# A fused cross-attention and expert block: some 128x128 transposes leave TensorE, are done as 32x32 blocks on VectorE and put in place through DRAM; PSUM banks come from one table, and each engine has a new order

## The reference

```python
# layer 1, on hidden = layernorm(x)
q = hidden @ Wq.T + bq;  k = ctx @ Wk.T + bk;  v = ctx @ Wv.T + bv     # 16 heads of 32
scores = clip(q @ k.T / sqrt(32), -50, 50);  masked keys to -10000, then clipped again
probs = softmax(scores);  probs = probs / (sum(probs) + 1e-8)
delta = clip(residual_scale, 0, 0.3) * (probs @ v @ Wo.T + bo)
x = x + (delta - mean) / sqrt(var + 1e-5) * ln_gamma + ln_beta
# layer 2, on n = layernorm(x)
weights = softmax(n @ router_w.T)                     # 8 experts, the best 2 are kept
h = einsum('bth,eih->beti', n, down_w);  a = silu(h)  # 16 hidden values for each expert
x = x + sum over the kept experts of weight * (a @ up_w.T)
```

## Time and profile before

| what | before |
|---|---|
| time, median of 3 runs (lowest to highest) | 189.34 us (188.48 to 189.62) |
| span of the profiled execution, first to last instruction | 187.4 us |
| TensorE busy | 180.4 us (96% of the span) |
| VectorE busy | 126.2 us (67%) |
| ScalarE busy | 111.4 us (59%) |
| GpSimd busy | 89.2 us (48%) |
| granted TensorE clock | 1.00 throughout |
| hardware DMA queue, share of 16 engines | 31.4% |

### The profile page before, as it was taken

One profiled execution on the slowest core, in us unless ns is written; L12 is line 12 of the kernel. 1 busy time (PEld: TensorE's weight loads), 2 busy tenths in 40 slices (PEclk: granted clock), 3 DMA queues, 4 the chain that ended last, 5 costly groups with the idle time before them and its releaser, 6 DMA issues.

```text
span 187.4 us, 3699 instructions
## 1 busy us (share of the span) xinstructions
PE 180.4 (96%) x1308; PEld 135.8 (72%) x1308; DVE 126.2 (67%) x294; ACT 111.4 (59%) x231; POOL 89.2 (48%) x149
## 2 busy tenths in 40 slices
PE   7999999889999999999999999999999999999972
...
GB/s 167 308 396 166 310 380 297 1 3 87 157 13 10 149 195 0 14 115 0 0 0 17 126 112 3 2 2 17 114 14 112 3 75 37 3 106 119 170 95 297
DMA packets 12290, 19.66 MB, mean 105 GB/s; under 512 B 2416, under 2 KB 4464, under 8 KB 12272
## 3 DMA queue, kind: packets, MB, share of 16 engines
q1 hardware_dynamic: 12272, 19.43, 31.4%
...
## 4 chain that ended last, share of the span: by engine, by line
PE 91%; DVE 4%; ACT 2%; issue 1%; POOL 0%; ACTq 0%; POOLq 0%
PE ps_r L434 52%; PE ps_v L434 8%; PE ps_t L459 8%; PE ps_r L513 5%; PE ps_v L540 4%; PE ps_v L527 4%; PE ps_r L489 4%; PE ps_v L499 4%; PE ps_v L590 3%; DVE xs L1175 2%; ACT stage L767 2%; ACT q_sb L753 0%; DVE hidt_lo L1063 0%; DVE hidden L1166 0%; ACT hidden L806 0%
## 5 line engine op out<-in xcount | busy, mean ns | idle before, releaser
L434 PE MATMUL ps_r<-wo_hi,attt_hi 128*128 128x512 f32 x64 | 26.3, 411 | 0.0
L434 PE MATMUL ps_r<-hst_hi,wq_hi 128*128 128x512 f32 x64 | 25.9, 404 | 0.4 <-ACT stage L767 0.4
L434 PE MATMUL ps_r<-hst_hi,wq_lo 128*128 128x512 f32 x64 | 25.3, 395 | 0.0
L434 PE MATMUL ps_r<-wo_hi,attt_lo 128*128 128x512 f32 x64 | 25.3, 395 | 0.0
L434 PE MATMUL ps_r<-hst_lo,wq_hi 128*128 128x512 f32 x64 | 25.2, 394 | 0.0
L434 PE MATMUL ps_r<-wo_lo,attt_hi 128*128 128x512 f32 x64 | 25.2, 394 | 0.0
L1445 POOL TENSOR_TENSOR xs<-xs,beta_bc 128x512 f32<-128x512 f32 x16 | 21.2, 1346 | 5.5 <-DMA beta_bc<-beta 5.5
L1449 POOL TENSOR_TENSOR attt_lo<-wk,attt_hi 128x512 fp32r<-128x512 f32 x16 | 21.2, 1335 | 4.4 <-ACT attt_hi L780 4.4
L747 ACT ACTIVATE hs<-xs,ln_bias,ln_rstd 128x512 f32<-128x512 f32 x16 | 12.7, 812 | 14.9 <-POOL ln_bias L1437 14.9
L1101 DVE TENSOR_SCALAR stage<-stage,exp_max 128x1024 f32<-128x1024 f32 x16 | 15.0, 935 | 9.0 <-ACT stage L767 8.7
L767 ACT ACTIVATE stage<-ps_r 128x1024 f32<-128x1024 f32 x16 | 16.1, 1025 | 5.4 <-PE ps_r L513 5.4
...
## 6 DMA issues: line engine op xcount, KB each, us to landing
...
```

What stands on the lines that cost most here:

```text
L434: last = pe.matmul(dst, w, m, start=start and i == 0, stop=stop and i == n - 1, skip_group_check=unseen)
```

## The change

Three things change together.

1. Batches 2 and 3 no longer have `hs_transpose`, and the pairs of tiles in `MOVED` (batches 0, 1 and 2, whole) no longer have `x1_transpose`. In their place VectorE turns each 32x32 block of the tile (`hs_turn`, `x1_turn`, one instruction a tile, from SBUF to SBUF). A block then still stands in the wrong group of 32 partitions. SP writes the turned tiles to DRAM (`hs_send`, 1 MB for a batch; `x1_send`, 512 KB for a pair) and reads them back in four DMAs, one for each 32 partitions (`hs_fetch`, `x1_fetch`), which puts the groups in place. ScalarE then makes `hst_hi` from SBUF, and GpSimd, not VectorE, makes `hst_lo`; `x1t` is copied by ScalarE from the fetched tiles.
2. The eight PSUM banks are one table, `BANKS`: each string is one bank, with its uses in order. Every kind has semaphores of its own for full and free.
3. The lists of all five engines are written anew. `spread` is cut in `spread_out` and `spread_in`, and small per-tile results have a slot for each batch, which takes two kinds of wait away from ScalarE (`projected_squares`, `x1_squares`).

```diff
+BANKS = (
+    "K0 Q01 S02 S06 Q13 S14 Q21 W03 Q30 S26 W12 S32 S36 W23 W30 U11 U22 U33",
+    "K1 Q02 S03 S07 S10 S15 Q22 Q23 S20 Q31 S27 W13 S33 S37 U00 W31 U12 U23",
+    "K2 Q03 S04 Q11 S11 S16 W00 S21 W10 Q33 S30 S34 W21 U02 W33 U20 U31",
+    "K3 S00 S05 Q12 S12 S17 W01 S22 S24 W11 S31 S35 W22 U03 U10 U21 U32",
+    "h01 h03 Q00 S01 Q10 S13 Q20 W02 S23 S25 Q32 W20 U01 W32 U13 U30",
+    "V0 h11 s00 v01 m0 s10 v11 s20 v21 f00 f02 a00 v30 v33 f12 f21 n30 f30 a21 a31",
+    "V1 h12 s01 v02 s11 v12 s21 v22 f01 s30 s31 v31 f10 f13 a10 f22 n31 a20 n33 f33",
+    "h00 h02 h10 h13 v00 v03 v10 v13 v20 v23 f03 a01 v32 f11 f20 a11 f23 n32 f31 f32 a30",
+)
+
+MOVED = ((0, 0), (0, 1), (1, 0), (1, 1), (2, 0), (2, 1))
+
+MOVED_HS = (2, 3,)
+
+LOW_ON_VECTOR = ()
+
...
+        hs_turned = sb("hs_turned", [P, KC * S])
+        x1_turned = sb("x1_turned", [P, 2, 2 * H])
+        hs_of = hs_turned[:, :].rearrange("p (q c t r) -> p t c q r", q=4, c=KC, t=NT)
+        x1_of = x1_turned[:, :, :].rearrange("p j (q c t r) -> p j t c q r", q=4, c=KC, t=2)
+
+        hs_back = hs[:, :, :].rearrange("p q (c t r) -> p q c t r", c=KC, t=NT)
+
+        x1_fetched = x1_turned[:, :, :].rearrange("p j (q n) -> p j q n", q=4)
+        x1_back = x1_turned[:, :, :].rearrange("p j (q c t r) -> p j t c q r", q=4, c=KC, t=2)
 
...
+            def hs_send(b):
+
+                sp.wait_ge(hs_turn_ok, NT * (MOVED_HS.index(b) + 1))
+                sp.dma_start(hs_scratch[:, :], hs_turned[:, :]).then_inc(hs_sent, 16)
+
+            def hs_fetch(b):
+                sp.wait_ge(hs_sent, 16 * (MOVED_HS.index(b) + 1))
+                for a in range(4):
+                    sp.dma_start(hs[32 * a:32 * (a + 1), :, :], hs_blocks[:, :, a, :]).then_inc(hs_moved, 16)
+
+            def x1_send(b, j):
+
+                sp.wait_ge(x1_turn_ok, 2 * (MOVED.index((b, j)) + 1))
+                sp.dma_start(x1_scratch[j, :, :], x1_turned[:, j, :]).then_inc(x1_sent[j], 16)
+
+            def x1_fetch(b, j):
+                sp.wait_ge(x1_sent[j], 16 * (b + 1))
+                for a in range(4):
+                    sp.dma_start(x1_fetched[32 * a:32 * (a + 1), j, :, :], x1_blocks[j, :, :, a, :]
+                                 ).then_inc(x1_moved[j], 16)
 
             def store(b, t):
-                sp.wait_ge(u_free, ring_r.count(f"U{b}{t}"))
...
+            hs_send(2)
+            spread_out(0, 0)
+            spread_in(0, 0)
+            hs_fetch(2)
             load(3)
-            spread(1, 1)
-            spread(2, 0)
-            spread(2, 1)
-            spread(3, 0)
-            spread(3, 1)
+            spread_out(0, 1)
+            spread_in(0, 1)
+            hs_send(3)
+            hs_fetch(3)
+            spread_out(1, 0)
+            spread_out(1, 1)
+            spread_in(1, 0)
+            spread_in(1, 1)
...
                 pe.wait_ge(hs_ok, NT * b + t + 1)
-                transposes(f"h{b}{t}", chunks(hs, t))
+                transposes(f"h{b}{t}", chunks(hs, t), h_full)
...
                 if m == 0:
-                    pe.wait_ge(hst_ok, ring_t.count(f"h{b}3"))
+                    dve, pool = hs_low(b + 1)
+                    pe.wait_ge(hst_ok, dve)
+                    if pool:
...
             def hs_hi(b, t):
                 if b:
-                    act.wait_ge(mm_full, ring_r.full(f"Q{b - 1}3"))
-                hi(f"h{b}{t}", hst_hi[:, t, :, :], hst_hi_ok)
+                    act.wait_ge(q_full, banks.count(f"Q{b - 1}3"))
+                if b not in MOVED_HS:
+                    hi(f"h{b}{t}", h_full, hst_hi[:, t, :, :], hst_hi_ok)
+                else:
+                    act.wait_ge(hs_moved, 64 * (MOVED_HS.index(b) + 1))
+                    act.copy(hst_hi[:, :, :, 32 * t:32 * (t + 1)].rearrange("p t c r -> p c t r"), hs_back[:, t, :, :, :]
+                             ).then_inc(hst_hi_ok, 1)
...
             def x1_out(b, t):
-                hi(f"n{b}{t}", x1t[:, t, :, :], x1t_ok)
+                if b:
+                    act.wait_ge(f_full, NT * (b - 1) + t + 1)
+                j = t // 2
+                if (b, j) in MOVED:
+                    act.wait_ge(x1_moved[j], 64 * (b + 1))
+                    act.copy(x1t[:, t, :, :].rearrange("p c (q r) -> p c q r", q=4), x1_back[:, j, t % 2, :, :, :]
+                             ).then_inc(x1t_ok, 1)
+                else:
+                    hi(f"n{b}{t}", n_full, x1t[:, t, :, :], x1t_ok)
...
             def hs_lo(b, t):
-                lo(f"h{b}{t}", hst_lo[:, t, :, :], hst_hi[:, t, :, :], hst_hi_ok, NT * b + t + 1,
-                   hst_ok)
+                if b not in MOVED_HS:
+                    lo(f"h{b}{t}", hst_lo[:, t, :, :], hst_hi[:, t, :, :], hst_hi_ok, NT * b + t + 1, hst_ok)
+                else:
+                    dve.wait_ge(hst_hi_ok, NT * b + t + 1)
+                    of_quarter = slice(32 * t, 32 * (t + 1))
+                    dve.tensor_tensor(hst_lo[:, :, :, of_quarter].rearrange("p t c r -> p c t r"), hs_back[:, t, :, :, :],
+                                      hst_hi[:, :, :, of_quarter].rearrange("p t c r -> p c t r").bitcast(F32),
+                                      ALU.subtract).then_inc(hst_ok, 1)
+
+            def hs_turn(b, t):
+
+                dve.wait_ge(hs_ok, NT * b + t + 1)
+                if MOVED_HS.index(b):
+                    dve.wait_ge(hs_moved, 64 * MOVED_HS.index(b))
+                dve.transpose(hs_of[:, t, :, :, :], hs[:, t, :]).then_inc(hs_turn_ok, 1)
+
+            def x1_turn(b, t):
+
+                j = t // 2
+                dve.wait_ge(x1_ok, NT * b + t + 1)
+                if b:
+                    dve.wait_ge(x1t_ok, NT * (b - 1) + 2 * j + 2)
+                dve.transpose(x1_of[:, j, t % 2, :, :, :], xs[:, NT * b + t, :]).then_inc(x1_turn_ok, 1)
 
...
+            def hs_lo(b, t):
+                pool.wait_ge(hst_hi_ok, NT * b + t + 1)
+                of_quarter = slice(32 * t, 32 * (t + 1))
+                pool.tensor_tensor(hst_lo[:, :, :, of_quarter].rearrange("p t c r -> p c t r"), hs_back[:, t, :, :, :],
+                                   hst_hi[:, :, :, of_quarter].rearrange("p t c r -> p c t r").bitcast(F32),
+                                   ALU.subtract).then_inc(hst_pool_ok, 1)
...
             tile_stats(2, 2)
+            tile_stats(2, 3)
+            clip(0, 0)
             hs_lo(1, 0)
             hs_lo(1, 1)
-            clip(0, 0)
+            hs_lo(1, 2)
             clip(0, 1)
-            hs_lo(1, 2)
             hs_lo(1, 3)
-            centre_experts()
+            hs_turn(2, 0)
+            hs_turn(2, 1)
+            hs_turn(2, 2)
+            hs_turn(2, 3)
+            reciprocals(0, 0)
+            centre_wo(2)
+            centre_wo(3)
             clip(0, 2)
-            reciprocals(0, 0)
             clip(0, 3)
-            tile_stats(2, 3)
```

939 lines of the change are left out of this document (475 added, 464 removed), and 4 rows, old and new, of the table RING_R.

## The result

| | before | after |
|---|---|---|
| time, median (lowest to highest) | 189.34 us (188.48 to 189.62) | 198.36 us (196.74 to 199.44) |
| ratio, 95% interval | | 1.048 (1.042 to 1.053) |
| profiled span | 187.4 us | 197.1 us |
| TensorE idle within the span | 7.0 us | 18.8 us |
| time lost to a lower granted clock | 0 | 7.4 us |

Slower by 4.8%, where I had forecast 2.6% faster. The last two rows are sums over slices of 1 us: what TensorE was not busy, and each slice's length times what its granted clock lacked of 1.00. Further down, a median is over all runs of a kernel, and a ratio leaves out runs over 1.5% longer than its fastest one (3 of e5's ten, 2 of e17's four, one each of e3's four and e10's six).

The account below looks back on a forecast made before the run. TensorE bounds the kernel, VectorE its end: `project(3, 3)` at 168.84 − 10.3 − 3.0 + 3.1 + 2.0 = 160.6, plus 3.5 + 15.7 + 2.7 gives a span of 182.5, plus 1.9 gives 184.4 us; range 179.5 to 190.5.

Parts of the forecast that it names:

- a microsecond of TensorE work taken away is a microsecond won: First matmul to 177.2 us: the chain hardly leaves TensorE, so removed work counts in full if no other engine is awaited.
- 10.3 us in full: Twenty transpose groups off TensorE: ten at 0.59, eight at 0.44, 0.9 for two more, all ahead of `project(3, 3)`.
- the term 3.1 + part of 2.0: New TensorE waits: 3.1 us before `scores(1, 1)` for batch 2's trip, 2.0 us for the other trips and short waits.
- Batch 2's own wait: Before `scores(1, 1)`: TensorE asks at 56.5, ScalarE frees the banks at 59.6, a wait of 3.1 us, bounds 0 and 6.
- hidden with a cover of 1 us: Batch 3's trip: tiles back by 77.0, `hs_lo(3, 3)` ends near 87, `query(3, 0)` comes at 88.3, so no wait.
- My own last sentence: Sign of being wrong: a first large wait at batch 3's queries or ScalarE's x1 copies means the order's covers set the loss.
- The first stretch, "even": Behind `query(0, 3)`, which ends at 33.8: `query(1, 0)` starts at 40.3 instead of 41.3, with 0.9 us of means still to do.
- The end: After `project(3, 3)` at 160.6 VectorE decides: 3.5 us to the last residual's end, 15.7 of VectorE work, 2.7 of store.
- My sign of it: Last 20 us: VectorE over 90% busy would show the forecast right.
- GpSimd's ten microseconds "are no bound": GpSimd takes eight `hs_lo` at 1.335 us, 10.7 us, to some 100 in all; that total is not a bound.
- the rival of dear transposes: Block transposes on VectorE cost more than one cycle an element; decides from 1.4 us a turn, 193.2 at 2.0; chance 0.11.
- The rival "trips cost double": DRAM trips: late turns delay SP's queue, waits of 6 us at batch 2 and 2 at batch 3's queries, 189.3; chance 0.14.

Follow-up runs that it names:

- e5: Changed kernel without the DRAM round trips of batches 2 and 3 (hs), their queries made from tiles turned within blocks only; 191.77 us, ratio 1.007.
- e17: Changed kernel with no DRAM trip (hs or x1), eight `hs_lo` back on VectorE, two centring steps later; 193.96 us, ratio 1.023, runs spread.
- e3: Changed kernel without send and fetch of batch 2, its queries made from tiles turned within blocks only; 195.63 us, ratio 1.029.
- e10: Kernel before with two x1 pairs, (0, 1) and (1, 0), turned by VectorE and moved through DRAM; 191.54 us, ratio 1.012.
- e16: Kernel before with 16 groups of transposes (eight hs, eight x1) left out and nothing in their place; 187.68 us, ratio 0.991.
- e15: Kernel before with the eight x1 transpose groups of batches 0 and 1 left out, nothing in their place; 189.26 us, ratio 0.999.
- e14: Kernel before with the eight hs transpose groups of batches 2 and 3 left out, nothing in their place; 188.45 us, ratio 0.994.
- e8: Changed kernel with VectorE's first two centring steps of the output weights moved behind `reciprocals(0, 0)`; 197.98 us, ratio 1.045.
- e2: Changed kernel with `hs_lo(1, 0)` moved ahead of two statistics and a clip in VectorE's list; 199.44 us, ratio 1.053.
- e1: Changed kernel with filler matmuls, results never read, in TensorE's three longest waits; 197.45 us, ratio 1.041.
- e4: Changed kernel with all eight `hs_lo` of batches 2 and 3 on VectorE instead of GpSimd; 194.78 us, ratio 1.028.
- e7: Changed kernel without the DRAM trips of the x1 tiles, projections reading the turned tiles themselves; 198.02 us, ratio 1.044.

## Why the prediction was wrong

**The step that failed first is "a microsecond of TensorE work taken away is a microsecond won".** I credited 10.3 us in full from the chain's 91%. In the old order e16 priced 16 of the 20 groups at 1.8 us instead of my 8.2, e15 eight x1 groups at nothing measurable (3.5 in my sum), e14 eight hs groups at 1.1 (4.7). These sums use the flat prices of the expectations, 0.44 and 0.59; the pieces of the chain give 4.1 and 4.3. The small worth is shown for the old order. For the new one e5 and e17 say no more than that 20 fewer groups did not make it fast, and why it is not faster without its trips stays open. I had given the condition myself ("if no other engine has to be waited for") and then took small waits for proof of it. A wait of 0.19 us behind a transpose says that ScalarE was ready 0.19 us after the transposes ended, so nothing can be won by ending them earlier. I took it as a sign that the pair counts in full (0.9 us).

**The trips of hs**: the term 3.1 + part of 2.0 stands against 4.1 points, 7.7 us (e5). Batch 2's own wait had the right place, releaser and size (3.29), the size by luck: the trip began 2.6 us late and took 1.1 us longer, and TensorE asked for `scores(1, 1)` at 60.2 and not at 56.5, so that two errors of nearly 4 us cancelled. What I mis-sized is the rest: batch 3, "hidden with a cover of 1 us", came back 6.7 us after my time, and a fetch took 7.8 us where my 7.6 was for the spread and the fetch together. Then `projected_squares` was late with it, as I had said it would be without the cover. My own last sentence named this case: the order's covers, not the first trip alone.

**The first stretch, "even".** It was a wait of 3.23 us. I had followed TensorE's list there and not VectorE's, where a late `bv`, eight statistics and a centring step of 1.42 us (0.49 without GpSimd beside it) stand ahead of `hs_lo(1, 0)`. Shrinking it gave 0.3 points, within the intervals (e8), or nothing (e2).

**The end** held in the main; the loss came ahead of it.

```profile
172.94 0.40 PE L471 MATMUL ps<-wo_hi,attt_lo 128*128 128x512 f32 x1
...
175.74 0.75 DVE L1175 SCALAR_TENSOR_TENSOR xs<-cen,d_rstd,xs 128x512 f32<-128x512 f32 x1 [0.28 <-POOL d_rstd L1528]
...
188.98 3.67 DVE L1224 TENSOR_TENSOR xs<-ps,xs 128x512 f32<-128x512 f32 x6
```

`project(3, 3)` ended at 173.3 where I had 160.6. From there on it is 3.2 us to the last residual's end (forecast 3.5), 16.2 us to VectorE's last operation (15.7) and 4.4 us to the end of the last store (2.7; e1 and e4 have 2.9). So 12.7 of the 14.6 us missed in the span lie ahead of the end. My sign of it was wrong: VectorE was busy for 72% of the last 20 us, not for over 90%. I had also priced VectorE's operations at their durations of before, and by their means clip, `residual` and the first step of the gate ran 18 to 35% longer.

**GpSimd's ten microseconds "are no bound"** was right for GpSimd and wrong for its neighbour: e4, 2.0 points in the order with the trips.

**What held**: the block transpose (0.67 to 0.70 for 0.65), so the rival of dear transposes falls; the x1 trips in the new order (e7); 1228 matmuls; a send of 1 MB in 3.8 us. The rival "trips cost double" had the mechanism that comes nearest, and its 189.3 still rested on the full credit. The half clock I had not considered; filling the holes, which took away 4.7 of its 7.4 us of deficit, gave 0.7 points at most (e1). One slip in the bounds: by its row the reciprocal takes 5.6 times as long for an element as `hs_lo`, not four times; the 3.8 us for a tile are right.

No version that computes the reference is faster than the kernel before. What freeing TensorE of these 16 groups gave in its order is 1% (0.6 to 1.3), before any price of the other way.
